# Weight pieces loaded between the stores, a first GRU state by twelve matmuls, step temporaries moved off the staged gates, and a weight chunk by one transfer

## The reference

```python
B, S, H = hidden_states.shape          # 8, 100, 256; G = 8 * 128 = 1024
h0 = hidden_states.mean(axis=1) @ ctx_w.T + ctx_b
xw = hidden_states @ gru_w_ih.T        # (8, 100, 3072)
def step(h, xw_t):
    hw = h @ gru_w_hh.T                # (8, 1024) x (1024, 3072)
    xr, xz, xn = jnp.split(xw_t, 3, axis=-1)
    hr, hz, hnn = jnp.split(hw, 3, axis=-1)
    r = jax.nn.sigmoid(xr + hr)
    z = jax.nn.sigmoid(xz + hz)
    n = jnp.tanh(xn + r * hnn)
    h_new = (1.0 - z) * n + z * h
    return (h_new, h_new)
_, hs = jax.lax.scan(step, h0, jnp.swapaxes(xw, 0, 1))
...
expr = (hidden_states @ expr_w.T).reshape(B, S, E, D)
```

## Time and profile before

| | |
|---|---|
| median of 3 runs | 3145.64 us (3142.97 to 3148.93) |
| profiled execution, its own time | 3167.93 us |
| span of the profile | 3166.1 us |
| TensorE busy | 2786.7 us (88%) |
| VectorE busy | 1784.5 us (56%) |
| ScalarE busy | 694.7 us (22%) |
| DMA queue q1, share of 16 engines | 23.0%, 230.35 MB |
| chain that ended last | PE 49%, DVE 31%, issue 6%, ACT 6%, DMA 5% |

### The profile page before, as it was taken

The page is one execution under the profiler, slowest core; times in us unless marked ns, Lnnn a source line. Parts: engine busy times, 40 slices in busy tenths (PEclk is TensorE's granted clock), DMA queues, the critical chain, the costliest instruction groups (busy, mean ns, idle before and its releaser), DMA issues.

```text
span 3166.1 us, 78551 instructions
## 1 busy us (share of the span) xinstructions
PE 2786.7 (88%) x32325; PEld 1799.1 (57%) x32325; DVE 1784.5 (56%) x5591; ACT 694.7 (22%) x1851; POOL 291.2 (9%) x681
## 2 busy tenths in 40 slices
PE   6888999899988999998988997888888888888887
PEld 4554456579765555554655664555555555555577
DVE  4545435421146666467466441477877778777743
ACT  2331133311122444310013431111111111111211
POOL 2112211020221000000211100000000000000111
PEclk9989989999998999999999998999999999999999
DMA  4000000079530000457111007311111111111176
GB/s 150 1 1 1 8 27 15 9 273 328 178 121 1 1 1 1 142 186 236 59 32 24 2 32 321 105 21 26 22 24 25 26 25 22 24 25 26 29 263 236
DMA packets 210667, 241.29 MB, mean 76 GB/s; under 512 B 152285, under 2 KB 178634, under 8 KB 199306
## 3 DMA queue, kind: packets, MB, share of 16 engines
q1 hardware_dynamic: 206446, 230.35, 23.0%
q0 software_dynamic: 3968, 7.56, 0.7%
HBM read 188.93 MB, written 56.21 MB: 77 GB/s over the span
## 4 chain that ended last, share of the span: by engine, by line
PE 49%; DVE 31%; issue 6%; ACT 6%; DMA 5%; SPq 2%; POOL 1%; DVEq 0%; POOLq 0%; ACTq 0%
PE banks L948 4%; PE banks L1323 4%; PE banks L641 4%; DVE arena L2387 3%; PE banks L1130 3%; PE banks L841 2%; PE banks L582 2%; PE banks L1194 2%; PE banks L1206 2%; PE banks L1369 2%; PE banks L970 2%; ACT arena L1719 2%; PE banks L988 1%; PE banks L994 1%; DMA arena<-whh 1%
## 5 line engine op out<-in xcount | busy, mean ns | idle before, releaser
L1323 PE MATMUL banks<-arena 128*32 128x384 bf16 x19200 | 834.6, 331 | 146.4 <-DVE arena L2350 139.6
L1323 PEld LDWEIGHTS banks<-arena 128*32 128x32 bf16 x19200 | 513.8, 98 | 464.9 <-DVE arena L2350 208.0
L1719 ACT ACTIVATE arena<-arena 128x64 f32<-128x64 f32 x200 | 51.3, 256 | 791.8 <-DVE arena L2392 762.3
L1130 PE MATMUL banks<-arena 128*128 128x400 f32 x512 | 176.9, 508 | 14.5 <-DMA arena<-hh 13.0
L641 PE MATMUL banks<-XNT,arena 128*128 128x400 f32 x384 | 149.9, 532 | 9.2 <-ACT XNT L1445 3.8
L948 PE MATMUL banks<-arena 128*100 128x256 f32 x512 | 138.7, 425 | 16.1 <-ACT XNT L1445 5.4
L1130 PEld LDWEIGHTS banks<-arena 128*128 128x128 f32 x512 | 98.3, 193 | 93.2 <-DMA arena<-hh 15.6
L2387 DVE STREAM_TRANSPOSE arena<-banks 128x384 f32<-128x384 f32 x200 | 112.0, 560 | 57.6 <-PE banks L1323 30.7
L1919 DVE TENSOR_REDUCE arena<-banks 100x4 f32<-100x1444 f32 x64 | 106.3, 1660 | 59.1 <-PE banks L794 58.9
L2671 POOL TENSOR_TENSOR rstd<-rstd 100x3 f32<-100x3 f32 (+1 forms) x120 | 23.3, 194 | 1250.8 <-DVE rstd L1874 1244.5
L841 PEld LDWEIGHTS banks<-arena 32*121 32x121 f32 x1536 | 101.1, 188 | 58.0 <-ACT arena L1545 35.7
(11 more groups left out here) (403 smaller groups left out, 4644.1 us busy)
## 6 DMA issues: line engine op xcount, KB each, us to landing
arena<-fc SPq DMA_DIRECT2D x22, 1024.0 KB, 4.8
arena<-pj SPq DMA_DIRECT2D x22, 1024.0 KB, 5.1
arena<-gu SPq DMA_DIRECT2D x21, 1024.0 KB, 5.0
whh_parts<-arena SPq DMA_DIRECT2D x32, 576.0 KB, 3.1
arena<-whh_parts SPq DMA_DIRECT2D x32, 576.0 KB, 14.7
arena<-whh SPq DMA_DIRECT2D x128, 96.0 KB, 3.2
arena<-dn SPq DMA_DIRECT2D x21, 512.0 KB, 4.1
xw<-arena SPq DMA_DIRECT2D x4, 2400.0 KB, 8.7
```

The costliest lines, as they stand in the source:

```text
L1130: last = nc.tensor.matmul(u[:, 0:HALF], w, x[:, half * HALF:(half + 1) * HALF], start=i == 0, stop=i == len(parts) - 1)
L1323: last = nc.tensor.matmul(banks[32 * j:32 * j + 32, 2 * c + i, 0:384], hs_tops[:, 1 - i, ub, :], whh[:, ub, j, c, part, :], start=opens an ...
L1719: nc.scalar.activation(rz[:, c], pre[:, c], ACT.Sigmoid).then_inc(sem["rz_done"], 1)
```

## The change

Five edits:
- A chunk of `whh` is loaded by one transfer whose read side is j, q, n (4 x 32 x 768) and whose write side is 128 x 768.
- `ctx_w` and `ctx_b` are loaded as they stand, in two transfers for twelve. The first state is made with `mean` (padded to 32 columns) as the stationary operand and `cw` as the moving one, four groups of three matmuls with 256 columns, and VectorE brings it into place with a transpose for a copy.
- The pieces of blocks 1, 2, 3 and 7 are loaded in portions of two or three between the seven `shown` stores.
- The temporaries of a GRU step lie at `AT_GRU` = 43136, off `staged[0]`. The inputs of steps 0 and 1 come by three loads each ahead of the pieces of block 7, and by a VectorE copy out of `staged[0]` for the fourth part. The inputs of odd steps lie in `const` (over the window mask).
- `load_x` and the wait for the last gates' store move accordingly: VectorE waits for `xw1` after the first ten steps.

```diff
+AT_GRU = AT_STATE - 1792
...
-        cw = block_of(AT_CW, 2, 8, P)
+        cw = block_of(AT_CW, 2, G)
...
-        g0 = AT_STAGED[0]
+        g0 = AT_GRU
...
-        xin = gru(2 * 192).rearrange("p (i g c m b) -> p i g c m b", i=2, g=2, c=2, m=12)
+        xin_at = (arena[:, AT_STAGED[0] - 192:AT_STAGED[0]], const[:, CONST["window"][0]:CONST["window"][0] + 192])
+        xin = [a_.rearrange("p (g c m b) -> p g c m b", g=2, c=2, m=12) for a_ in xin_at]
...
-        mean = block_of(AT_CW + 2 * G, 2, B)
-        cb = arena[0:1, AT_CW - G:AT_CW].rearrange("p (u n) -> p u n", u=8)
+        mean = block_of(AT_CW + 2 * G, 2, 32)
+        cb = arena[0:1, AT_CW - G:AT_CW]
...
-            for ub in range(8):
+            for j in range(4):
                 for kk in range(C):
-                    nc.tensor.matmul(u[:, ub * B:(ub + 1) * B], cw[:, kk, ub, :], mean[:, kk, :],
+                    nc.tensor.matmul(u[32 * j:32 * j + 32, 0:256], mean[:, kk, :], cw[:, kk, 256 * j:256 * j + 256],
                                      start=kk == 0, stop=False, skip_group_check=True)
-                last = nc.tensor.matmul(u[:, ub * B:(ub + 1) * B], cb[:, ub, :], ones[0:1, 0:B], start=False, stop=True, skip_group_check=True)
+                last = nc.tensor.matmul(u[32 * j:32 * j + 32, 0:256], ones8, cb[0:1, 256 * j:256 * j + 256],
+                                        start=False, stop=True, skip_group_check=True)
...
+            step(nc.vector.memset(mean[:, :, :], 0.0))
...
-            emptied(nc.vector.tensor_copy(hs[:, 1, :, 0:B], take()[:, 0:8 * B].rearrange("p (u b) -> p u b", u=8)))
+            emptied(nc.vector.transpose(hs[:, 1].rearrange("p u r -> p (u r)"), take()[:, 0:256]))
...
+            n.wait("a_evac", n.got("a_evac"))
+            for i in range(2):
+                nc.vector.tensor_copy(xin[i][:, 1, 0], staged[0][:, :, :, i]).then_inc(sem["l_x%d" % i], 16)
             settle()
-            dve.wait_ge(sem["xw1"], 32)
...
+            dve.wait_ge(sem["xw1"], 32)
             dve.wait_ge(sem["l_expr"], 160)
...
-            whh_rows = dram["whh"].rearrange("(v q) (j c o n) -> v q j c o n", v=4, j=4, c=2, o=4)
+            whh_rows = dram["whh"].rearrange("(v q) (j c o n) -> v c o j q n", v=4, j=4, c=2, o=4)
...
-                for j in range(4):
-                    sp.dma_start(split_in[v % 2][32 * j:32 * j + 32], whh_rows[ub % 4, :, j, ub // 4, j_out, :]).then_inc(sem["l_split%d" % (v % 2)], 16)
+                sp.dma_start(split_in[v % 2], whh_rows[ub % 4, ub // 4, j_out]).then_inc(sem["l_split%d" % (v % 2)], 16)
...
-            for j in range(4):
-                sp.dma_start(cb[:, :, 32 * j:32 * j + 32], cb_rows[:, j]).then_inc(sem["l_cw"], 16)
-                for kk in range(C):
-                    sp.dma_start(cw[:, kk, :, 32 * j:32 * j + 32], cw_rows[:, kk, j]).then_inc(sem["l_cw"], 16)
+            load(cb, "ctx_b", "l_cw")
+            load(cw.rearrange("p k g -> p (k g)"), "ctx_w", "l_cw")
...
-            load_whh((1, 4, 5, 6))
+            load_whh((4, 5, 6))
...
-            load_whh((2, 3))
-            sp.wait_ge(sem["xw0"], 32)
-            load_whh((7,))
+            late = [(ub, j) for ub in (1, 2, 3, 7) for j in range(4)]
             for i in range(TILES):
...
                 sp.dma_start(shown[i * P:i * P + rows], expr_out[0:rows, i % 2]).then_inc(sem["e_out%d" % (i % 2)], 16)
+                for ub, j in late[16 * i // TILES:16 * (i + 1) // TILES]:
+                    if (ub, j) == (7, 0):
+                        sp.wait_ge(sem["xw0"], 32)
+                        sp.wait_ge(sem["xw1"], 16)
+                        for k in range(2):
+                            load_x(k, k, cells=((0, 0), (0, 1), (1, 1)))
+                    load_whh_part(ub, j)
...
             for i in range(2):
                 sp.wait_ge(sem["xw%d" % i], 32)
-            for k in range(2):
-                load_x(k, k)
+                sp.wait_ge(sem["l_x%d" % i], 64)
```

More of the change, by code:

```diff
@@ L239, in build @@
         held_down = block_of(held_at, 4, D)
-        shared_gu = block_of(AT_STATE - 2048, 2, 2, 512)
+        shared_gu = block_of(AT_STAGED[0], 2, 2, 512)
         up3 = arena[:, 14400:15200].rearrange("p (r t) -> p r t", r=2)
@@ L299, in build @@
         expr = XN[0:ROWS, G:2 * G]
-        lap_at = g0
+        assert g0 <= AT_STATE
+        lap_at = AT_STAGED[0] + 2048
         def lap_block(rows, n_):
@@ L338, in build @@
         region_il = lap_block(1, 24).bitcast(I32)
-        assert lap_at <= AT_STATE - 2048, lap_at
+        assert lap_at <= AT_GRU, lap_at
         ROW_RING = 7
@@ L2303, in split_weights @@
                 whole = x.rearrange("p (g c n) -> p c g n", g=3, c=2)
-                dve.wait_ge(sem["l_split%d" % (v % 2)], 64 * (v // 2 + 1))
+                dve.wait_ge(sem["l_split%d" % (v % 2)], 16 * (v // 2 + 1))
                 if v >= 2:
@@ L2334, in _ @@
             n.wait("a_evac", n.got("a_evac"))
+            step(nc.vector.memset(mean[:, :, :], 0.0))
             for kk in range(C):
-                last = nc.vector.tensor_reduce(mean[:, kk, :], XNT[:, kk, :].rearrange("p (b s) -> p b s", b=B), AX, ALU.add)
+                last = nc.vector.tensor_reduce(mean[:, kk, 0:B], XNT[:, kk, :].rearrange("p (b s) -> p b s", b=B), AX, ALU.add)
             step(last)
@@ L2384, in step_of @@
                     us = slice(4 * c, 4 * c + 4)
-                    x_of = lambda lo, hi: xin[:, i, :, c, lo:hi, :].rearrange("p g m b -> p m g b")
+                    x_of = lambda lo, hi: xin[i][:, :, c, lo:hi, :].rearrange("p g m b -> p m g b")
                     dve.wait_ge(sem["gates%d" % c], at_(2, i + 1))
@@ L3009, in _, with load_whh_part @@
                         store_split(v)
+            def load_whh_part(ub, j):
+                sp.dma_start(whh[:, ub, j].rearrange("p c s n -> p (c s n)"), whh_parts[4 * ub + j]).then_inc(sem["l_whh"], 16)
             def load_whh(blocks):
@@ L3014, in load_whh @@
                     for j in range(4):
-                        sp.dma_start(whh[:, ub, j].rearrange("p c s n -> p (c s n)"), whh_parts[4 * ub + j]).then_inc(sem["l_whh"], 16)
+                        load_whh_part(ub, j)
             def store_gates(g, c):
@@ L3021, in _ @@
             wih_rows = dram["wih"].rearrange("p (k j g c v u) -> p k j c g v u", k=2, j=4, g=3, c=2, v=4)
-            cw_rows = dram["ctx_w"].rearrange("p (k j v u) -> p k j v u", k=2, j=4, v=8)
-            cb_rows = dram["ctx_b"].rearrange("p (j v u) -> p j v u", j=4, v=8)
             def load_wih(c):
@@ L3051, in _, with load_x @@
             x_steps = xw.rearrange("(g c) p (s n) -> s g c p n", g=2, s=S)
[L3053 to L3059, removed]
+            def load_x(row, i, ahead=0, cells=((0, 0), (0, 1), (1, 0), (1, 1))):
+                for g, c in cells:
+                    src_ = x_steps[2 * ahead:S - 2 + 2 * ahead]
+                    sp.dma_start(xin[i][:, g, c].rearrange("p m b -> p (m b)"), src_[bass.ds(row, 1), g, c].rearrange("o p n -> (o p) n")
+                                 ).then_inc(sem["l_x%d" % i], 16)
             def store_h(row, i):
```

2 lines of the change are left out of this document (1 added, 1 removed).

## The result

| | before | after |
|---|---|---|
| median of 10 runs | 3152.59 us (3141.95 to 3160.82) | 3172.64 us (3164.77 to 3194.37) |
| profiled execution | 3167.93 us | 3190.35 us |
| split stretch: first block of `hh` on TensorE to the end of the last | 190.6 us | 238.1 us |
| turn: first unit of `xw` to the first half of step 5 turned on VectorE | 138.0 us | 117.9 us |

The change makes the kernel slower: ratio 1.0077, 95% interval 1.0049 to 1.0104, +20 us on the medians (+24 on the means, from which the ratio comes) against +21 forecast. The two profiled executions differ by 22.4 us of span: -6.6 ahead of the split stretch, **+47.5 in it**, +6.9 between the stretches, **-20.1 in the turn**, -5.3 after step 5.

A forecast was written before the change was run, and what follows sets the result against it. Bound by the chain chunk in, split, chunk out, hh in the split stretch, and by TensorE waiting on queued shown stores in the turn. +42 and -21 gave +21 us, 3167 us, range 3150 to 3190.

The forecast's parts named there:

- Four engines: Split stretch: the one chunk transfer, outer read count 4, uses only 4 of 16 DMA engines; +42 us, 6.4 us a chunk.
- Issue: Split stretch, time from split end to next chunk's data: one issue instead of four saves 1.6 us.
- Data: Split stretch, same time: 98.3 KB on each of four engines at 27.5 GB/s adds 3.4 us.
- Store on the same engines: Split stretch, same time: the new transfer stands behind the split chunk's store, +1.0 us (0 to 1.3).
- Rival 1: Write side's 128 rows decide, all 16 engines carry the transfer: split stretch -3, turn -24, 3122 us; chance 0.12.
- Rival 3: Split stretch: four engines, each faster alone than in crowded rows; 5.4 us a chunk, +12 and -21, 3137 us; chance 0.05.
- Rival 2: Turn gives nothing: pieces arrive as late as the GRU starts today; +42, 3188 us; chance 0.05.
- The turn: From last attention to GRU: piece order, clock and moved temporaries together gain 21 to 22 us (ends 14 and 27).
- Start of the GRU: Turn: all 32 weight pieces have landed at 1985 instead of 2001.7, so the GRU starts 16.7 us sooner.
- The first state: Turn: twelve matmuls of 256 columns take 5.2 us instead of 9.7, on a path something else closes.
- The small waits: Turn: TensorE's 17.1 us of standing still between expression tiles become some 4 to 6 us.
- Behind the start: Turn, first GRU steps: low clock +2.5, second step sooner -4.9, its matmuls at full clock -2.6 us.

The follow-up runs named there:

- e5: Changed kernel with whh laid out in HBM so that a chunk's read side is 8 x 16 x 768, still one transfer; 3137.10 us, ratio 0.9961.
- e2: Kernel before the change with only the load of a whh chunk made one transfer (read side 4 x 32 x 768); 3193.96 us, ratio 1.0133.
- e4: Changed kernel with whh laid out in HBM so that a chunk's read side is 16 x 8 x 768, still one transfer; 3117.37 us, ratio 0.9883.
- e6: e3 with the weight pieces back in their old order, 12 of them ahead of the first shown store; 3126.75 us, ratio 0.9916, turn 131.0 us.
- e1: Changed kernel with the load of a whh chunk put back to four transfers of 32 rows; 3129.14 us, ratio 0.9943.
- e3: Changed kernel with whh laid out in HBM so that a chunk's read side is 128 flat rows of 768, still one transfer; 3118.80 us, ratio 0.9879.
- e8: e3 with the first state made as before (48 records of 8 columns, ctx_w in twelve transfers); 3114.02 us, ratio 0.9878, turn 119.5 us.
- e10: e3 with the xn_rows store and the first expressions' loads moved behind the last gates' store; 3113.10 us, ratio 0.9867, turn 111.4 us.
- e9: e3 with the four weight pieces of block 1 back ahead of the gates' store; 3119.74 us, ratio 0.9890, turn 119.8 us.
- e7: e3 with the wait for the last gates' store back before the first GRU step and step inputs loaded behind it; 3112.48 us, ratio 0.9873.

## Why the prediction was right

**Four engines.** Right. Every sign came: DMA share 0.48, every split behind a wait, single blocks from the eighth on with waits of 5 to 7 us, the end of the stretch at 1581.7 (forecast 1583). The profile shows no landing time for the new load, nor for e5's, so that sign couldn't be read; the packets show the four engines in its place. The term was +42 and is +47.5 in after, +51.3 in e2; a chunk 6.54 us (6.4), L 9.24 (9.0). The steps inside came near, too:

- Issue: -1.6 forecast; 0.55 us instead of 2.3, so -1.76.
- Data: +3.4 forecast at 27.5 GB/s an engine. Measured, 32 packets of 0.121 us are 3.87 us, and the last quarter's two packets before are 0.24: +3.6.
- Store on the same engines: +1.0 forecast; what is left, 9.24 - 6.18 + 1.76 - 3.6, is 1.2. That it is the store's is argued from the estimate above and wasn't tried apart.

So the full row's rate was nearer (25.4 GB/s a packet) than that of the 1 KB row; the 22 GB/s that the steps between e4, e5 and after give have other transfers' packets in them.

**Rival 1** was wrong in its condition (the write side's 128 rows don't decide) and right in its price: with 16 outer rows on the read side the stretch is 3.6 us shorter than before (forecast -3), L 5.92 (5.9 to 6.1). Its total was -24; the two stretches of e4 give -25.4, its plain runs -34 on the medians with an interval of some -52 to -21. Its bound, a chunk under 5.7 us, is bracketed: e5 at 5.45 us is faster than before, after at 6.54 slower. **Rival 3** falls: a packet takes 0.12 us with 4 engines as with 16. **Rival 2** falls with e6: the order of the pieces is worth 14.7 us.

**The turn.** -21 to -22 forecast, -20.1 measured, -21.4 in e1. Start of the GRU: -14.6 against -16.7; in e3, whose first twelve units run at before's clock, -17.2. The first state takes 6.1 us, not 5.2: the matmul of `ones8` with 256 columns costs 0.54 us for two records and the product 0.98 for four, 0.25 to 0.27 a record, and not 0.22. The queue moved 26.6 MB in 76.8 us; less the 2 us of latency that the forecast also takes off this is 0.356 MB/us against 0.365 (e3: 0.367). The small waits are 7.3 us, not 4 to 6. Behind the start -5.5 against -5.0. In sum the gain of the order is confirmed by e6 (14.7 against 16.7 - 2.5 = 14.2), and that of the temporaries as well (7.0 against 4.9 + 2.6 = 7.5). That the clock takes back 2.5 us of the one and gives 2.6 of the other was forecast rightly: 2.7 and 2.2 are what the steps of e3 and before show. One step of the text was wrong: that the -4.5 us of the first state lie "on a path that something else closes". e8 shows 3.2 of 3.6 us coming through in the new order; in e6's old order they don't.

## What to carry over

Before you join transfers, write down the outermost count of both sides: four small loads that use all DMA engines beat one large load whose read side begins with a 4, by 1.5 us a chunk here, and laying the data out in HBM as it is read turned the same edit from +47 into -13 us. Where stores that free a buffer and loads that are needed later share one queue, deal the loads out between the stores; the gain is the standing still of the engine, and its new bound is the bytes of the queue before the last load, so what isn't needed before it goes behind. An edit's worth depends on what else is late: waiting for the gates' store costs 7.0 us in one order and 2.5 in the other, where the low clock of the first step has already cost as much.

## What the hardware did that was not expected

*The clock after a short pause.* Windows of 5 us, 1.1 and 1.5 us behind the start of the GRU, of e3 (behind a pause of 4.13 us) and of e10 (behind 3.60 us):

```profile
1970.00:1975.00 5.00, 5.00 (x76) 2.61 (x68) 0.00 (x0) 0.00 (x0) 0.00 (x0) 0.56 0.67 280
```

```profile
1959.00:1964.00 5.00, 4.50 (x110) 2.88 (x102) 1.30 (x5) 0.11 (x1) 0.00 (x0) 1.00 0.81 300
```

The first (granted clock 0.56) runs nearly all at 1.2 GHz, the second (1.00) at 2.4; the first half-step is turned 7.8 us after the start in one and 5.1 in the other. The length of the pause doesn't sort the runs: e5 keeps the clock after 4.00 us, e9 loses it after 4.00, after itself after 3.13. What sorts them stays open. Of the 2.7 us some 1.7 reach the end of the turn (e5 114.6, e3 116.3), so a single execution's turn is uncertain by that much. The first step is slow in e7, e8 and e9 as it is in e3, so their differences from e3 aren't of this kind.

*The time of untouched code.* From the start of the profile to the first block of `hh` the program has the same work in all kernels shown and takes 1322.8 (e2, e9) to 1350.2 us (before); between the two stretches it takes 369.9 (e5) to 386.1 us (e3), 370.1 in before and 377.1 in after. The first of these ranges, 27 us, is more than the turn's half of the change is worth. The differences of span that a single pair of profiles shows are no measurement of such a change; stretches between two marks are, and ten plain runs. The cause of the 27 us was not looked for.
